# Attention heads divided through DRAM rows instead of PE transposes, with the output product two periods later

## The reference

```python
x = x + 0.5 * ffn(layernorm(x))        # w1, w2 rounded to -1, 0, 1; exact gelu; 256 -> 1024 -> 256
x = x + attention(layernorm(x))        # x: (16, 256, 256)
x = x + 0.5 * ffn(layernorm(x))        # the same weights again

def attention(x):
    q, k, v = (x @ W.T, split into 16 heads of 16, for W in (Wq, Wk, Wv))
    q, k = rope(q), rope(k)
    scores = where(causal, q @ k.T / 4, -inf)
    return concat_heads(softmax(scores) @ v) @ Wo.T
```

## Time and profile before

| | |
|---|---|
| median of 3 runs | 603.38 us (602.57 to 603.78) |
| profiled execution, first to last instruction (span) | 600.8 us |
| first feed-forward part | about 0 to 150 us |
| attention | about 150 to 477 us |
| second feed-forward part | about 477 to 601 us |
| PE, DVE, ACT, POOL busy in the span | 567.2, 458.9, 345.2, 229.3 us |

### The profile page before, as it was taken

How to read it: one execution, slowest core, us unless ns; L and a number is a source line. 1 busy time by engine, 2 the same in 40 slices (tenths; PEclk the granted TensorE clock), 3 DMA queues, 4 the chain that set the end, 5 groups by cost and what they waited for, 6 DMA issues and landing times.

```text
span 600.8 us, 17866 instructions
## 1 busy us (share of the span) xinstructions
PE 567.2 (94%) x6596; PEld 496.4 (83%) x6596; DVE 458.9 (76%) x928; ACT 345.2 (57%) x610; POOL 229.3 (38%) x446
## 2 busy tenths in 40 slices
PE   1999999999789999999999999999888999999998
PEld 1789999999668888888888888888665788999997
DVE  5977777779797978879788788877562777777765
ACT  2765454546246666776667766567545655455453
POOL 6383333332665354444544445434141033333310
PEclk9999999999999999999999999999989999999999
DMA  6530000000987567654576546765400011111111
GB/s 221 199 112 6 0 0 0 0 0 1 257 219 207 167 164 208 172 157 146 166 204 177 158 139 175 197 186 159 138 2 3 1 36 35 35 35 35 35 35 36
DMA packets 71190, 63.45 MB, mean 106 GB/s; under 512 B 4178, under 2 KB 64370, under 8 KB 71154
## 3 DMA queue, kind: packets, MB, share of 16 engines
q1 hardware_dynamic: 69970, 62.81, 36.1%
q10 hardware_dynamic: 1184, 0.14, 0.2%
HBM read 33.03 MB, written 29.36 MB: 104 GB/s over the span
## 4 chain that ended last, share of the span: by engine, by line
PE 82%; DVE 10%; DMA 3%; ACT 2%; issue 1%; POOL 1%; SPq 1%; ACTq 0%; DVEq 0%
PE bank L173 18%; PE bank L537 18%; PE bank L1065 13%; PE bank L673 6%; PE bank L1060 6%; PE bank L1121 5%; PE bank L1196 4%; PE bank L1161 3%; PE bank L156 2%; PE bank L1124 2%; PE bank L1134 2%; DVE mx L863 2%; DVE g_lo L257 2%; PE bank L1184 1%; DMA w1f<-w1t 1%
## 5 line engine op out<-in xcount | busy, mean ns | idle before, releaser
L863 DVE TENSOR_REDUCE mx<-bank 128x2 f32<-128x512 f32 (+1 forms) x192 | 118.7, 684 | 31.3 <-PE bank L1065 31.2
L240 ACT ACTIVATE g<-bank,b1c 128x512 f32<-128x512 f32 x128 | 88.0, 690 | 65.6 <-PE bank L173 62.5
L537 PE MATMUL bank<-w2q,g_hi 128*128 128x256 f32 x512 | 124.4, 284 | 1.3 <-DVE g_lo L257 0.9
L537 PE MATMUL bank<-w2q,g_lo 128*128 128x256 f32 x512 | 122.5, 280 | 0.0
L985 ACT ACTIVATE probs<-bank 128x512 f32<-128x512 f32 x192 | 111.2, 597 | 11.9 <-PE bank L1065 4.4
L537 PEld LDWEIGHTS bank<-w2q,g_hi 128*128 128x128 f32 x512 | 96.5, 188 | 2.9 <-DVE w2q L375 1.1
L537 PEld LDWEIGHTS bank<-w2q,g_lo 128*128 128x128 f32 x512 | 96.5, 188 | 0.6
L315 POOL TENSOR_TENSOR res<-res,b2h 128x1024 f32 (+1 forms) x16 | 38.3, 2394 | 133.0 <-DVE xn L147 128.9
L257 DVE TENSOR_TENSOR g_lo<-g,g_hi 128x512 fp32r<-128x512 f32 x128 | 82.8, 689 | 3.1
L173 PE MATMUL bank<-xt_hi,w1q 128*128 128x512 f32 x240 | 77.3, 404 | 2.0 <-DVE xt_lo L167 2.0
L173 PE MATMUL bank<-xt_lo,w1q 128*128 128x512 f32 x240 | 76.4, 400 | 0.0
(11 more groups left out here) (129 smaller groups left out, 1170.1 us busy)
## 6 DMA issues: line engine op xcount, KB each, us to landing
qk_slots<-parts SPq DMA_DIRECT2D x32, 384.0 KB, 3.6
q<-qk_slots SPq DMA_DIRECT2D x32, 384.0 KB, 4.0
k<-qk_slots SPq DMA_DIRECT2D x32, 384.0 KB, 4.5
qk_slots<-parts SPq DMA_DIRECT2D x32, 256.0 KB, 3.4
res<-x SPq DMA_DIRECT2D x8, 512.0 KB, 3.6
qk_slots<-parts SPq DMA_DIRECT2D x32, 128.0 KB, 3.2
out<-res SPq DMA_DIRECT2D x7, 512.0 KB, 2.9
w1f<-w1t SPq DMA_DIRECT2D x2, 512.0 KB, 6.1
```

The source lines that it names most:

```text
L240: nc.scalar.activation(g[:, f, :], of[:], ACT.Gelu, bias=b1c[:, f:f + 1]).then_inc(g_ready, 1)
L537: last = nc.tensor.matmul(to[:, 0:D], part[:, f, t * P:(t + 1) * P], w2q[:, f, :], start=f == 0 and part is g_hi, stop=f == FC - 1 and par ...
L863: nc.vector.tensor_reduce(o, i, AX.X, ALU.max).then_inc(s_done, 1)
```

## The change

The heads are no longer turned on PE. `copy_heads` still copies the bank to SBUF. SP stores this copy whole to DRAM (256 KB a half, the 16 features, the sum and 15 repetitions of it for each of eight heads). It loads back the sums of the element as a 128 by 32 tile (`load_den`, 64 bytes a row and half), DVE takes all reciprocals at once, and SP stores them (`store_rden`). A period later SP loads the numerators as rows in the layout that the output product wants (256 KB) and the reciprocals repeated for the 16 features of each head (256 KB, `load_output`). DVE multiplies the two in one instruction, ACT and DVE split it, and PE multiplies by Wo for element p-2 instead of p-1. OT and ANT are gone. The output products of the last two elements run in chunks 0 and 1 of the second feed-forward part, into bank 5. Rows of Wo are put in the new order on the host.

The order around it changes as well. On DVE `reciprocals` and `normed_heads` stand ahead of `maxima(p, 1)` and `low_att` stands in its middle. On ACT `copy_att` stands in the middle of `exponentials(p, 1)`. `copy_heads(p, 0)` also waits for the stored reciprocals (`rden_out`). PV waits for ACT's copy alone. The masks are one tile, broadcast over heads when PE reads them. The loops of the attention stage run over periods 3 to 10 instead of 1 to 10, and more chunks of the second feed-forward part are written out. Some tiles move; the fences and constant rows lie in the space of `by_cos` until DVE first writes it.

```diff
+        def reciprocals(dve, p):
+            dve.wait_ge(den_in, 32 * p.p)
+            if p.has(-2):
+                dve.wait_ge(rden_out, 16 * (p.p - 1))
+            nc.vector.reciprocal(rden[:], den[:]).then_inc(den_s, 1)
+        def normed_heads(dve, p):
+            dve.wait_ge(heads_in, 16 * (p.p - 1))
+            dve.wait_ge(rden_in, 16 * (p.p - 1))
+            nc.vector.tensor_tensor(att[:], att[:], rden_rows[:], ALU.mult).then_inc(normed, 1)
+        def copy_att(act, p):
+            act.wait_ge(normed, p.p - 1)
+            nc.scalar.copy(att_t[0][:].rearrange("p k s -> p (k s)"), att[:]).then_inc(att_hi_s, 1)
+        def output(pe, p, to=mixed[1]):
+            pe.wait_ge(att_lo_s, p.p - 1)
+            if to is o_bank:
+                pe.wait_ge(o_copied, 2 * BATCH)
+            elif p.has(3):
+                pe.wait_ge(v_done, p.p + 4)
+            else:
+                pe.wait_ge(wo_done, p.p - 1)
...
+            def store_heads(p, h):
+                sp.wait_ge(o_copied, 2 * p.p + h)
+                sp.dma_start(heads_dram[p.p - 1 + h, 1 - h].rearrange("j r s -> (j r) s"), o_sb[:]).then_inc(o_stored, 16)
+            def load_den(p):
+                sp.wait_ge(o_stored, 32 * p.p)
+                for half in range(2):
+                    sp.dma_start(den[:, half, :], heads_dram[p.p - 1, half, :, HD, :]).then_inc(den_in, 16)
+            def store_rden(p):
+                sp.wait_ge(den_s, p.p)
+                sp.dma_start(rden_dram[p.p - 1].rearrange("h (p c) -> p h c", p=P), rden[:]).then_inc(rden_out, 16)
+            def load_output(p):
+                b = p.p - 2
+                if p.known and p.p > BATCH:
+                    sp.wait_ge(att_lo_s, p.p - 2)
+                    sp.wait_ge(rden_out, 16 * (p.p - 1))
+                sp.dma_start(att[:], heads_dram[b, :, :, 0:HD, :]).then_inc(heads_in, 16)
+                sp.dma_start(rden_rows[:], rden_dram[b].rearrange("h (j s) -> h j s", j=4).unsqueeze(2)
+                             .broadcast_to([2, 4, HD, KC * SEQ])).then_inc(rden_in, 16)
             def step(p, h):
+                if p.has(-1) if h == 0 else p.has(0):
+                    store_heads(p, h)
+                if h == 0 and p.has(-2):
+                    load_output(p)
                 if p.has(2):
                     load(p, h)
+                if p.has(-1):
+                    if h == 0:
+                        load_den(p)
+                    else:
+                        store_rden(p)
                 if h == 1 and p.has(3):
                     store(p, 0, Q_RUNS)
...
                 else:
+                    if p.has(-1) and not last:
+                        reciprocals(dve, p)
+                    if p.has(-2) and not last:
+                        normed_heads(dve, p)
+                    if p.has(1):
+                        maxima(p, 1, range(3))
+                    if p.has(-2) and not last:
+                        low_att(dve, p)
+                    if p.has(1):
+                        maxima(p, 1, range(3, 6))
...
             def copy_heads(p, h):
-                j = 2 * p.p + h - 1
-                act.wait_ge(pv_done, j + 1)
-                nc.scalar.copy(o_sb[:].rearrange("p g s -> p (g s)"), o_bank[:]).then_inc(o_copied, 1)
+                act.wait_ge(pv_done, 2 * p.p + h)
+                if p.has(-1):
+                    act.wait_ge(o_stored, 16 * (2 * p.p + h - 1))
+                if h == 0 and p.has(-2):
+                    act.wait_ge(rden_out, 16 * (p.p - 1))
+                nc.scalar.copy(o_sb[:], o_bank[:]).then_inc(o_copied, 1)
...
                 if h == 1:       
-                    if p.has(-1):
-                        copy_att(p)
+                    if p.has(0):
+                        exponentials(p, 1, range(3))
+                    if p.has(-2) and not last:
+                        copy_att(act, p)
+                    if p.has(0):
+                        exponentials(p, 1, range(3, 6))
...
                 if p.has(-1) or h: 
-                    pe.wait_ge(normed, 2 * p.p + h)
+                    pe.wait_ge(o_copied, 2 * p.p + h)
...
                 if h == 0:
-                    if p.has(-1):
-                        OT(p, 0)
                 else:
-                    if p.has(-1):
-                        ANT(p)
                     if p.has(3):
                         V(p)
-                    if p.has(0):
-                        OT(p, 1)
                     if p.has(4, 2):
                         XT(p)
-                    if p.has(-1):
-                        WO(p)
+                    if p.has(-2) and not last:
+                        output(pe, p)
...
+                            if late and c == 0 and f == FC - 3:
+                                of_last.reciprocals(dve)
+                        if late:
+                            of_last.normed_heads(dve, c)
                         low_part(dve, gc, FC - 1, first)
```

More of the change, by code:

```diff
@@ L110, in macaron_kernel @@
         by_cos, by_sin, rot, rest = (sb(n, [P, 2, 2 * SEQ]) for n in ("by_cos", "by_sin", "rot", "rest"))
-        parts = [sb(f"parts{p}", [P, 2, PARTS, 2 * SEQ], BF16) for p in range(2)]
+        few = by_cos[0:PARTS, 0, :].bitcast(BF16)
+        fence_q, fence_k, minus_rows = (few[:, i * SEQ:(i + 1) * SEQ] for i in range(3))
+        rows_in = [sem(f"att_rows_in{p}") for p in range(2)]
+        parts = [sb("parts0", [P, 2, PARTS, 2 * SEQ], BF16)]
+        den, rden = (sb(n, [P, 2, KC * SEQ * 4 // P]) for n in ("den", "rden"))
+        o_sb, att, rden_rows = (sb(n, [P, KC * SEQ]) for n in ("o_sb", "att", "rden_rows"))
         turning = Turning(scratch, by_cos, by_sin, rot, rest, parts,
@@ L379, in turn_first @@
                     def turn_first():
+                        for rows in rows_in:
+                            dve.wait_ge(rows, 48)
                         for t in range(2):
@@ L412, in chunk @@
                         dve.wait_ge(xb_ready, gc + 1)
+                        if late:
+                            of_last.low_att(dve, c)
                         for t in range(CT):
@@ L528, in chunk @@
                                 continue
+                            if phase == 1 and not opening and f == 3:
+                                pe.wait_ge(wo_done, BATCH + (0 if isinstance(c, int) and c == 1 else 1))
                             if opening:
@@ L580, in macaron_kernel @@
         before = feed_forward(0)
-        attend = attention(nc, sem, banks, turning, res, (wqk_hi, wqk_lo), (wv_hi, wv_lo), (wo_hi, wo_lo), cos_t, sin_t, ident, ident_b, mask_qk, mask_kq, minus_rows,
+        attend = attention(nc, sem, banks, turning, res, (wqk_hi, wqk_lo), (wv_hi, wv_lo), (wo_hi, wo_lo), cos_t, sin_t, ident, ident_b, mask_qk, mask_kq, att_t, o_sb, att, rden_rows, den, rden, rden_dram, heads_dram, rows_in, minus_rows,
                            fence_q, fence_k, pad_cols, stats, normaliser, mean, rstd, xn, xt_hi, xt_lo,
@@ L665 @@
 Stage = namedtuple("Stage", "sync gpsimd vector scalar tensor helpers")
+LastOutput = namedtuple("LastOutput", "reciprocals normed_heads copy_att low_att output add_output")
 Turning = namedtuple("Turning", "scratch by_cos by_sin rot rest parts qk_ready rope_s rot_s top_s rest_s mid_s low_s stored")
@@ L691, in store_turned, with attention @@
           .then_inc(turning.stored[par][t], 16)
-def attention(nc, sem, banks, turning, res, wqk, wv, wo, cos_t, sin_t, ident, ident_b, mask_qk, mask_kq, minus_rows,
+def attention(nc, sem, banks, turning, res, wqk, wv, wo, cos_t, sin_t, ident, ident_b, mask_qk, mask_kq, att_t, o_sb, att, rden_rows, den, rden, rden_dram, heads_dram, rows_in, minus_rows,
               fence_q, fence_k, pad_cols, stats, normaliser, mean, rstd, xn, xt_hi, xt_lo,
@@ L776, in sync @@
             periods(sp.Fori, step)
+            load_output(Period(BATCH + 1))
         def gpsimd(pool):
@@ L1021, in step @@
             def step(p, h):
+                last = p.known and p.p == BATCH
+                if last and h == 0:
+                    for f in (2, 3):
+                        then.gelu(act, CHUNKS, f, banks[f])
+                    then.cast_by_act(act, CHUNKS, 2)
                 if p.has(-1) if h == 0 else p.has(0):
                     copy_heads(p, h)
-                if p.has(0):
-                    exponentials(p, h)
+                if h == 0 and p.has(0):
+                    exponentials(p, 0)
                 if h == 1:
-                    if p.has(-1):
-                        copy_att(p)
+                    if p.has(0):
[4 more added lines that the diff above has]
+                        exponentials(p, 1, range(3, 6))
                     if p.has(3):
@@ L1046, in step @@
                     then.cast_by_act(act, CHUNKS, 0)
-                if p.known and p.p == BATCH and h == 0:
-                    for f in (2, 3):
-                        then.gelu(act, CHUNKS, f, banks[f])
-                    then.cast_by_act(act, CHUNKS, 2)
```

203 lines of the change are left out of this document (83 added, 120 removed).

## The result

The change made the kernel slower: 701.52 us (median of 4 runs, 699.92 to 707.35) against 603.58 us (4 runs, 602.57 to 603.84). The ratio is 1.1637, with an interval from 1.1586 to 1.1689. The prediction said 631 us and a range up to 655. The direction and the place of the stall came as said, but the loss is 98 us and not 28. The profiled execution spans 701.0 us, 100.2 more than before.

What follows compares the result with a forecast made beforehand. PE, busy 94% of the span, was taken as the bound. The 600.8 us span plus 25.2 for attention stalls and 1.8 at the end gave 627.8, with 2.6 to the median 630.4, rounded to 631; range 598 to 655.

Steps and rivals of the forecast that it cites:

- Half 0 without OT: Half 0 of an attention period: removing OT from PE's path wins 0.59 us.
- I count nothing: Half 1: removing ANT (0.59 us) wins nothing, since an equally long chain through ACT's `copy_v` remains before WO.
- The place of the stall: Half 1: `reciprocals` on DVE, ahead of the maxima, waits for sums whose heads' store SP can't issue before t1+4.3.
- D = 11.4: Sums land 11.4 us after t1, the period's start of S, behind queued transfers at 285 GB/s; lower bound 9.2.
- The next t1 is at D+9.0: Next period's S units start 9.0 us after the sums land; D of 11.4 gives a 20.4 us period.
- Sum of a period: Attention periods 2 to 13: 1.6 us from D plus 0.5 for statistics, 2.1 us a period, 25 us in all.
- `rden_out` hidden by 0.3 us: `copy_heads(p, 0)`: stored reciprocals land at about D+8.6, before PV ends at D+8.9, so the wait costs nothing.
- The end: Last attention periods win 2.6 us, transposes of chunk 1 come 1.5 later, output products add 2.9: together +1.8 us.
- Few engines: Rival, chance 0.18: loads with eight or four outer rows use that many DMA engines; D + 3.2, 669 us.
- No stall: Rival, chance 0.18: sums land by t1+8.4, attention wins 7.1 us, the end adds 1.8: 598 us.
- Light stall: Rival, chance 0.12: D at 9.2 or 9.7, periods about even, +1.8 us at the end: 603 to 612 us.
- main case: Attention stalls each period on the sums' late landing, D between 10.2 and 12.8: 612 to 650 us, chance 0.52.

Runs made afterwards that it cites:

- e8_free_rows: The changed kernel with all maxima and exponentials of half 1 ahead of the DMA-dependent work, and `att` and `rden_rows` loaded over 16 outer rows: 611.0 us.
- e12_mask: The kernel before with only the 128 by 128 masks and their broadcast read: 603.7 us, ratio 1.0004.
- e7_free: The changed kernel with all six maxima and exponentials of half 1 ahead of product, `low_att`, reciprocals and `copy_att`; transfers unchanged: 623.0 us.
- e2_spread: The changed kernel with the new loads over more outer rows, 32 for the sums, 16 for `att` and `rden_rows`: 692.3 us.
- e6_denfirst: The changed kernel with the sums' loads issued on SP ahead of the q and k loads: 665.0 us.
- e3_filler: The changed kernel with 20 unused 512-column products on PE before S(p, 9), once a period in periods 1 to 12: 691.1 us.
- e11_ends: The free-order, 16-row version of 611.0 us with the last two elements' work later in chunks 0 and 1 of the last feed-forward: 605.0 us.
- e10_half0: The changed kernel with product and output product a period later in half 0, 16-row loads, sums ahead of q and k, and later end work: 598.3 us.
- e4_den: The changed kernel with only the sums' loads over 32 outer rows and the reciprocals stored by two DMAs: 707.7 us, ratio 1.1734.

## Why the prediction was wrong

By its own steps:

- **Half 0 without OT.** Right in kind: 8.34 us after against 8.81, 0.47 won where 0.59 was said. "I count nothing" for ANT in half 1 was right: even without the stall, in e8_free_rows, half 1 is no shorter.
- **The masks**, taken at nothing: right (e12_mask).
- **The place of the stall.** Right: `reciprocals` in half 1, PE stopped by the ring of maxima, the heads' store at t1+4.1. Taking the waits for DMAs from ahead of the maxima removes most of it, and all of it with faster rows (e7_free, e8_free_rows). "Needed by t1+8.4" is t1+8.1 by the text's own terms; nothing hangs on it.
- **D = 11.4, with the statistics 11.9 on average.** This is the term that was mis-sized. Measured 14.55, 2.65 us more. I filled the engines from t1+4.9 to t1+10.4 without a gap at 285 GB/s. In fact they are half empty for 3 us, then run at 226 to 240 GB/s. Runs settle two shares. Of the measured D 0.9 us is the eight outer rows of `att` and `rden_rows` (e2_spread), which also leave the engines half empty. 2.3 us is the place behind q and k (e6_denfirst), which the prediction had in its sum as 2.7. The rest I only argue: longer issues on SP put the sums' loads at t1+7.6, and a slower pace for 1.5 MB would be worth 1.536/0.24 - 1.536/0.285 = 1.0 us. No run here takes the pace or SP's issues by itself.
- **"The next t1 is at D+9.0."** At full clock this is right to 0.5 us (9.2 to 9.5 in e3_filler, 9.3 to 9.4 in e6_denfirst, whose three periods with the predicted D took 20.6 to 20.7 us where the text said 20.4). After, it is D+11.7. The missing step is the granted clock. The text noted that a fall "would come on top" and gave it no price. It is 2.7 us a period, as much as the miss in D. The 2.85 us for the V product against 1.41 alone is 1.44 of it.
- **Sum of a period.** Said: 2.1 us over before. Measured: 7.55. The difference of 5.4 is 2.65 of D and 2.7 of clock, over eleven periods 60 of the 70 us that the median is off.
- **`rden_out` hidden by 0.3 us.** Nearly: 6.2 us in all of the span.
- **The end.** Said +1.8 us over three places. The end of attention took 4.4 us more to the last PV instead of 2.6 less. From there to the transposes of chunk 1 it was 14.2 us instead of 12.6 to 13, since the sums came 4.9 us after their issue at 567.04 and not 2.3. The output product of chunk 0 ran at a low clock (2.9 us against 1.43), and the rest of the second feed-forward part took 5.6 us more where 2.9 was said. With the order of e11_ends the end comes near the said +1.8: from period 13 on it takes 185.1 us, and before 183.7.
- **The rivals.** "Few engines" named a true mechanism at four times its size; its 669 us is nearer to the result than the forecast by luck, since its 3.2 us stood for 0.9, and even its range ends at 685. "No stall" needed D below 9.8, and the least that any period of after or of e6_denfirst shows is 11.2. "Light stall" fell as well. The main case's own range, 612 to 650 for D from 10.2 to 12.8, is 616 to 648 by the text's formula; the result lies outside either.

The loss is thus mainly one stall with two prices: how late the sums land, and the clock behind it. How the other 1.75 us of D's miss divide between SP's longer issues, the pace and whatever else stays open.

## What to carry to other kernels

Price a stall of PE twice: by its length, and by what runs at 1.2 GHz behind it. Here that second price (2.7 us) was as large as the mistake in the length. Never put an instruction that waits for a DMA ahead of the small rings that feed the busiest engine: the same loads, moved behind six maxima and spread over 16 rows, cost 7.5 us a period less. When two dependent transfers go by way of DRAM in one period, don't let anything on the path wait for them in that period: e10_half0, which uses the result a period later, is 5.2 us faster than before.

## What was not expected of the hardware

- Clock: with PE idle from 330.0, the granted clock was 1.00 until 332 and 0.50 from 333, and four us of full work later it was still 0.50. Even 2.2 us of idling behind a filler let it fall (0.62, then 0.52) once PE worked again (e3_filler), yet three stalls of 2.4 to 2.8 us in e6_denfirst left it at 1.00.
- DMA: two loads of eight outer rows left the engines at a share of 0.38 and 70 GB/s for one us between stretches of over 1.0; with 16 outer rows the same stretch had 0.71 and 121 GB/s. At shares of 1.02 and 1.03 the loads ran at 226 to 240 GB/s against 282 for the stores at 1.07.
- The sums, 8 KB a load, took 4.7 us to land in e2_spread, and spreading them alone over 32 outer rows, with the reciprocals' store in two DMAs, made the kernel 6 us slower (e4_den).
